# Cross attention layers of a decoder: scores for the row maxima of two heads per step, each head in its own half of the stack's rows; maxima moved in two transfers instead of three

## The reference

```
q = LN(x) @ Wq.T + bq ; k = ctx @ Wk.T + bk ; v = ctx @ Wv.T + bv      (no biases in L0)
scores = einsum('bhqd,bhkd->bhqk', q, k) / sqrt(8)      (L3: masked by a table)
out = softmax(scores) @ v ;  x = x + out @ Wo.T + bo
```

## Time and profile before

| | us |
|---|---|
| runs | 2594.87, 2597.32, 2603.39 |
| median of 3 runs | 2597.32 |
| profiled execution, own time | 2597.72 |
| its span | 2595.9 |
| PE busy | 2275.9 (88%) |
| DVE busy | 1563.2 (60%) |
| ACT busy | 1306.7 (50%) |
| mean granted TensorE clock | 0.933 of full |

### The profile page before, as it was taken

How to read it: one execution, slowest core, us unless ns; L and a number is a source line. 1 busy time by engine, 2 the same in 40 slices (tenths; PEclk the granted TensorE clock), 3 DMA queues, 4 the chain that set the end, 5 groups by cost and what they waited for, 6 DMA issues and landing times. The chain is left out here.

```text
span 2595.9 us, 48375 instructions
## 1 busy us (share of the span) xinstructions
PE 2275.9 (88%) x16585; PEld 1478.1 (57%) x16585; DVE 1563.2 (60%) x4614; ACT 1306.7 (50%) x3591; POOL 722.2 (28%) x996
## 2 busy tenths in 40 slices
PE   8879997789898599976889998887779999899989
PEld 5635544755555245543756766566747776466643
DVE  5667762246666778745366664553366775877730
ACT  5646661235556166652356676422235565466632
POOL 2232202444432522200633231234421121322100
PEclk8989998879999699997989999988989999899999
DMA  2123316220000133220600000265410001232100
GB/s 80 31 71 102 97 41 199 46 65 34 18 34 17 50 100 105 83 84 29 157 3 2 1 1 15 84 137 147 135 37 2 10 2 40 84 86 80 52 19 17
DMA packets 127203, 155.40 MB, mean 60 GB/s; under 512 B 22496, under 2 KB 90345, under 8 KB 125810
## 3 DMA queue, kind: packets, MB, share of 16 engines
q1 hardware_dynamic: 116850, 143.20, 19.3%
q0 software_dynamic: 7488, 7.78, 1.4%
q10 hardware_dynamic: 2624, 1.32, 0.3%
HBM read 117.96 MB, written 34.99 MB: 59 GB/s over the span
## 5 line engine op out<-in xcount | busy, mean ns | idle before, releaser
L540 ACT ACTIVATE L3x_p_ring<-L3x_ps_t 128x512 f32<-128x512 f32 x256 | 141.7, 599 | 101.2 <-PE L3x_ps_t L615 100.1
L442 DVE CUSTOM_DVE_ANT_0 L3x_ps_s<-L3x_ps_s,L3x_mask_q 128x512 f32<-128x512 f32 x256 | 170.1, 718 | 27.6 <-PE L3x_ps_s L596 26.3
L540 ACT ACTIVATE L1x_p_ring<-L1x_ps_t 128x512 f32<-128x512 f32 x256 | 138.0, 623 | 76.9 <-PE L1x_ps_t L613 76.8
L540 ACT ACTIVATE L0x_p_ring<-L0x_ps_t 128x512 f32<-128x512 f32 x256 | 138.0, 626 | 72.7 <-PE L0x_ps_t L613 72.6
L445 DVE TENSOR_REDUCE L0x_mx<-L0x_ps_s 128x2 f32<-128x1024 f32 x128 | 151.9, 1221 | 29.4 <-PE L0x_ps_s L596 29.0
L445 DVE TENSOR_REDUCE L1x_mx<-L1x_ps_s 128x2 f32<-128x1024 f32 x128 | 152.1, 1221 | 21.6 <-PE L1x_ps_s L596 20.4
L1087 ACT ACTIVATE L2a_probs<-L2a_ps_s,L2a_top 128x256 f32<-128x256 f32 x256 | 117.8, 472 | 78.6 <-DVE L2a_top L1022 78.5
L1087 ACT ACTIVATE L3a_probs<-L3a_ps_s,L3a_top 128x128 f32<-128x128 f32 (+1 forms) x256 | 104.0, 422 | 40.1 <-DVE L3a_top L1018 37.9
L613 PE MATMUL L3x_ps_t<-L3x_q_stack,L3x_k_stack 128*128 128x256 bf16 x512 | 120.3, 274 | 1.7 <-DMA L3x_q_stack<-L3x_m_rows 1.4
L615 PE MATMUL L3x_ps_t<-L3x_mask_k,const_ident_bf 128*128 128x256 bf16 x512 | 119.9, 274 | 0.0
L596 PE MATMUL L1x_ps_s<-L1x_k_stack,L1x_q_stack 125*128 125x512 bf16 x256 | 80.6, 397 | 16.3 <-PEq L98 11.8
(11 more groups left out here) (769 smaller groups left out, 6056.0 us busy)
## 6 DMA issues: line engine op xcount, KB each, us to landing
L2f_w_e<-L2f_in_w_e SPq DMA_DIRECT2D x23, 544.0 KB, 3.7
L0f_w<-L0f_in_w SPq DMA_DIRECT2D x32, 256.0 KB, 6.9
L1a_rk_wide<-L1a_rk_dram SPq DMA_DIRECT2D x8, 1024.0 KB
L1f_w<-L1f_in_w SPq DMA_DIRECT2D x32, 256.0 KB, 3.4
L0x_k_stack<-L0x_k_dram SPq DMA_DIRECT2D x84, 96.0 KB
L1x_k_stack<-L1x_k_dram SPq DMA_DIRECT2D x84, 96.0 KB
L3x_k_stack<-L3x_k_dram SPq DMA_DIRECT2D x84, 96.0 KB
kept_x<-ctxT SPq DMA_DIRECT2D x24, 256.0 KB, 3.2
```

Of the source, the lines that this page charges most:

```text
L442: last = dve.tensor_tensor_reduce(span, span, mask_q[:, t, :], 1.0, 2 * MASKED, ALU.add, ALU.max, accum_out=mx[:, t, k:k + 1])
L540: act.activation(p_ring[:, u % RING, j * BANK:(j + 1) * BANK], t_bank(o), ACT.Exp, scale=scale).then_inc(out["t"].sem, 1)
```

## The change

Heads are taken in pairs (h, h+4), one of an even quarter and one of an odd quarter. An even quarter's nine pairs of parts stay in rows 0 to 71, in another order, so that rows 0 to 63 hold all but the product of the two small parts. An odd quarter's stand in rows 56 to 127, so that rows 64 to 127 hold all but that product. Step `s` is now one t of two heads: a matmul over rows 0 to 63 and one over rows 64 to 127, both 128 by 512. There are as many of them. The maxima of an odd quarter's heads go into rows 0 to 2. `t` is as before.

```diff
+Q_SLOTS = (0, 1, 2, 0, 1)
+K_SLOTS = (2, 0, 1, 2)
+STACK_ROWS = (((0, 1, 1), (24, 2, 1), (48, 0, 1)), ((56, 2, 0), (80, 0, 0), (104, 1, 0)))
+MAX_ROWS = (P - 3, 0)
+
+def store_parts(eng, name, dram, parts, stored):
+    if name == "q":
+        eng.dma_start(dram[0:3].rearrange("i p k -> p i k"), parts[:]).then_inc(stored, 16)
+        eng.dma_start(dram[3:5].rearrange("i p k -> p i k"), parts[:, 0:2, :]).then_inc(stored, 16)
+    else:
+        eng.dma_start(dram[1:4].rearrange("i p k -> p i k"), parts[:]).then_inc(stored, 16)
+        eng.dma_start(dram[0:1].rearrange("i p k -> p i k"), parts[:, 2:3, :]).then_inc(stored, 16)
+
+def load_quarter(eng, name, stack, dram, par, quarter, stacked):
+    heads = slice(QUARTER * quarter, QUARTER * (quarter + 1))
+    for row, q_slot, k_slot in STACK_ROWS[quarter % 2]:
+        slot = q_slot if name == "q" else k_slot
+        eng.dma_start(stack[row:row + 24, par, heads], dram[slot:slot + 3].rearrange("i (d h) k -> (i d) h k", h=16)[:, heads]
+                      ).then_inc(stacked, 16)
...
-        m_stacked = [tally(f"m_stacked_{j}_", 3 * 16) for j in range(2)]
+        m_stacked = [tally(f"m_stacked_{j}_", 2 * 16) for j in range(2)]
...
-                        for i in range(3):
-                            sp.dma_start(q_stack[MAX_ROW + i:MAX_ROW + i + 1, par, heads],
-                                         m_rows[H * i + HALF * k:H * i + HALF * (k + 1), k]).then_inc(m_stacked[k].sem, 16)
+                        for odd in range(2):
+                            first = HALF * k + QUARTER * odd
+                            sp.dma_start(q_stack[MAX_ROWS[odd]:MAX_ROWS[odd] + 3, par, first:first + QUARTER],
+                                         m_rows[3 * QUARTER * odd:3 * QUARTER * (odd + 1), k]).then_inc(m_stacked[k].sem, 16)
...
-                        if k % QUARTER == 0 and b == 0:
-                            pe.wait_ge(prologue.stacked[k // QUARTER], 6 * 16)
-                        elif k % QUARTER == 0:
-                            wait_tally(pe, stacked[k // QUARTER], b, 6 * 16)
-                        for t in range(QT):
-                            last = pe.matmul(s_bank(o)[:, t, :], q_stack[0:MAX_ROW, par, k, t * P:(t + 1) * P], k_stack[0:MAX_ROW, par, k, :],
+                        for quarter in (k // QUARTER, k // QUARTER + 1):
+                            if k % HALF == 0 and b == 0:
+                                pe.wait_ge(prologue.stacked[quarter], 6 * 16)
+                            elif k % HALF == 0:
+                                wait_tally(pe, stacked[quarter], b, 6 * 16)
+                        first, t = first_of_pair(k), k % 2
+                        for j in range(2):
+                            rows, h = slice(j * P // 2, (j + 1) * P // 2), first + QUARTER * j
+                            last = pe.matmul(s_bank(o)[:, j, :], q_stack[rows, par, h, t * P:(t + 1) * P], k_stack[rows, par, h, :],
                                              start=True, stop=True)
...
-                            last = pe.transpose(t_bank(o).bitcast(BF16)[:, t * P:(t + 1) * P],
-                                                mparts[:, t, :, :].rearrange("p a h -> p (a h)"), const["ident_bf"][:])
+                            last = pe.transpose(t_bank(o).bitcast(BF16)[0:3 * HALF, t * P:(t + 1) * P],
+                                                mparts[:, k].rearrange("p c i h t -> p (c i h) t")[:, :, t], const["ident_bf"][:])
```

More of the change, by code:

```diff
@@ L268, in attention_cross @@
         v = sb("v", [P, 2, KT, H, 32])
[L269 to L272, removed]
+        mx = sb("mx", [P, 2, 2, QUARTER, QT])
+        mrest = sb("mrest", [P, 2, 2, QUARTER, QT])
+        mparts = sb("mparts", [P, 2, 2, 3, QUARTER, QT], BF16)
+        m_rows = sb("m_rows", [3 * HALF, 2, S], BF16)
         p_ring = sb("p_ring", [P, RING, 2 * BANK])
@@ L329, in load_stack @@
         def load_stack(eng, name, quarter, b):
[L331 to L337, removed]
+            stack, dram, stored = (q_stack, q_dram, q_stored) if name == "q" else (k_stack, k_dram, k_stored)
+            wait_tally(eng, stored, b, 32)
+            load_quarter(eng, name, stack, dram, b % 2, quarter, stacked[quarter].sem)
         with nc.Block() as block:
@@ L452, in _ @@
                             wait_tally(dve, full["m"], b, 0)
[L453 to L454 removed]
                         else:
                             wait_tally(dve, full["m"], b, 1)
[L457 removed]
+                        part = [mparts[:, k, :, i] for i in range(3)]
+                        dve.tensor_scalar(part[0], mx[:, k], -1.0, None, ALU.mult).then_inc(m_steps.sem, 1)
                         wait_tally(dve, m_steps, b, 4 * k + 1)
[L459 to L462 removed]
+                        dve.scalar_tensor_tensor(part[1], mx[:, k], -1.0, part[0], ALU.mult, ALU.subtract).then_inc(m_steps.sem, 1)
+                        dve.scalar_tensor_tensor(mrest[:, k], mx[:, k], -1.0, part[0], ALU.mult, ALU.subtract).then_inc(m_steps.sem, 1)
                         wait_tally(dve, m_steps, b, 4 * k + 3)
[L464 removed]
+                        dve.tensor_tensor(part[2], mrest[:, k], part[1], ALU.subtract).then_inc(m_steps.sem, 1)
                     if kind == "v" and qk_bias:
@@ L544, in _ @@
                         wait_tally(act, m_stacked[k], b, 0)
-                        act.activation(m_rows[:, k], t_bank(o).bitcast(BF16)[:, 0:S], ACT.Copy).then_inc(out["m"].sem, 1)
+                        act.activation(m_rows[:, k], t_bank(o).bitcast(BF16)[0:3 * HALF, 0:S], ACT.Copy).then_inc(out["m"].sem, 1)
                     if kind == "outputs":
@@ L657, in __init__ @@
         self.q_dram = nc.dram_tensor(name + "first_q_dram", [5, P, S], BF16)
-        self.k_dram = nc.dram_tensor(name + "first_k_dram", [3, P, KX], BF16)
+        self.k_dram = nc.dram_tensor(name + "first_k_dram", [4, P, KX], BF16)
         self.masks = masks
     def load_stack(self, eng, name, quarter):
-        heads = slice(QUARTER * quarter, QUARTER * (quarter + 1))
-        dram = self.q_dram if name == "q" else self.k_dram
-        for a in range(3):
-            rows = dram[a:a + 3] if name == "q" else dram[:]
-            eng.dma_start(self.stacks[name][24 * a:24 * a + 24, 0, heads], rows.rearrange("i (d h) k -> (i d) h k", h=16)[:, heads]
-                          ).then_inc(self.stacked[quarter], 16)
+        load_quarter(eng, name, self.stacks[name], self.q_dram if name == "q" else self.k_dram, 0, quarter, self.stacked[quarter])
 def attention_rows(nc, x_sb, const, w, cfg, ahead, follow, stacks, opening, prologue):
@@ L3614, in fill @@
                 def fill(name, par):
-                    rows = prologue.stacks[name][P // 2:P, par].rearrange("p h k -> p (h k)").bitcast(F32)
+                    rows = prologue.stacks[name][:, par].rearrange("p h k -> p (h k)").bitcast(F32)
                     words = two_ones if name == "k" else const["zero"]
-                    act.activation(rows, words[P // 2:P, 0:1].broadcast_to(list(rows.shape)), ACT.Copy).then_inc(filled, 1)
+                    act.activation(rows, words[:, 0:1].broadcast_to(list(rows.shape)), ACT.Copy).then_inc(filled, 1)
                 act.wait_ge(two_made, 1)
```

45 lines of the change are left out of this document (18 added, 27 removed).

## The result

The changed kernel took 2590.94 us (median of 11 runs, 2588.54 to 2593.77), the kernel before beside it 2597.19 (11 runs, 2593.71 to 2603.39). The ratio is 0.9981, 95% interval 0.9972 to 0.9989: 5 to 6 us less (4.9 by the ratio, 6.3 by the medians). The interval tells this from no change, though it is under the 0.3% that the prediction took as its bound. The profiled execution took 2589.7, its span is 2587.8 and its mean clock 0.936. The prediction had said 2590.0.

What follows compares the result with a forecast made beforehand. TensorE was taken to bound L3x throughout, TensorE and VectorE by turns L0x and L1x, with starts at reduced clock. Savings 2.2 + 2.7 + 2.7 = 7.6 us from 2597.7 gave 2590.1, stated as 2590.0; range 2586 to 2594.

Steps and rivals of the forecast that it cites:

- L0x and L1x: Steady batches of these layers: gain counts only where VectorE waits for TensorE; 0.17 us a batch, 2.7 us for 16.
- the starts: Layer starts at half clock: 1.35 us saved up to the first t, 1.3 behind it; together 2.7, bounds 0 and 5.
- L3x's gain: Steady batches of L3x, all TensorE: 0.27 us a batch saved, times 8 is 2.2 us; bounds 1.4 and 3.0.
- Step s: Between full-shape blocks, shape changes included: 0.42 us against 0.435, about 0.01 saved; right behind values 0.115 saved.
- free leaving: Rival: leaving the small shape costs nothing, each s saves 0.09 more; 21 us more, 2569 or part of it; chance 0.20.
- the full 2x: Rival: no change of shape costs; L3x saves 27 us, the others 21; some 2549; chance 0.05.
- the pair's weights: Rival: weights of the pair in s aren't hidden, 0.10 us more each; slower, 2616 to 2628; chance 0.09.
- m's way out: From m's 24-row transposes into t: 0.10 us or nothing; half taken, 0.05 each, two a batch.
- The clock: Layers' starts: a differing clock would prove the forecast wrong; rival that it rises later, 2597 to 2612, chance 0.08.
- The stack's quarters: First s of a half waits for two quarters' loads, expected free; the forecast is wrong if TensorE waits for one.
- Nothing comes through: Rival: in L0x and L1x the gain becomes longer waits for mparts and ScalarE; 2594 to 2600; chance 0.18.

Runs made afterwards that it cites:

- m_full: Changed kernel with m's transposes 128 columns wide again (24 of maxima, the rest zeros): 2589.01 us, ratio to the kernel before 0.9971.
- late_max: Changed kernel with one maximum a batch, the one waiting for the s right behind values, also waiting for the t that follows: 2593.29 us.
- before_m_first: Kernel before, with only the maxima's transfers issued by SP ahead of the six loads of a stack's quarter: 2594.46 us.
- after: The changed kernel in its first profile, no further edit: the profiled execution took 2589.7 us.
- after_again: The changed kernel profiled once more, no edit: 2594.84 us.

## Why the prediction was right, and where it wasn't

The time was right to a microsecond (2590.0 for 2590.94), the saving less so (7.6 for 5 to 6; the base was 0.5 above the later median), and the sum behind it least. Predicted were 2.2 for L3x, 2.7 for L0x and L1x, 2.7 for the starts. The traces give 0.2 for L3x behind its first `y`, 4.8 for L0x and L1x behind theirs, and 1.2 for the three starts up to it, which hold one and a half batches. L3x's gain did not come, L0x's and L1x's was nearly twice as large, and the starts' was half. That these errors of both signs nearly cancelled is luck.

- **Step s, right.** Predicted were 0.42 against 0.435, measured 0.426 against 0.435, and behind `values` 0.115 less predicted, 0.113 measured. The changes of shape eat the gain: free leaving (each step 0.09 cheaper) and the full 2x are out by L3x, whose period didn't fall, and the pair's weights are hidden for a bf16 follower (the next `t` comes 0.32 behind the pair and not 0.42).
- **m's way out, the term that was mis-sized.** Between 0.10 and nothing the prediction took half; it is 0.096, in full, as m_full shows. The price of nothing came from the earlier trace rows, from a group of fp32 transposes, which did not hold for these bf16 ones. The lower bound, 1.4 for L3x, was still too high, because of the next point.
- **x and v behind the pair, not in the sum.** The prediction priced what follows `s` by the `t` that follows; twice a batch it is a fp32 matmul. That a first fp32 matmul behind a change of shape can be 0.10 dearer stood in the earlier trace rows, and the prediction weighed it as a rival for the bf16 pair alone. With it L3x adds up: `s` 14 x 0.009 + 2 x 0.113 = 0.35 less; `m` twice 0.096 and 0.01 for the `t` behind it, 0.21 more; `x` 0.05 and `v` 0.10 more. Together that is +0.01, against +0.02 measured (33.117 to 33.133).
- **L0x and L1x, right mechanism, too small.** 0.17 a batch predicted, 0.32 and 0.33 measured. The step that failed is that `m` costs 2 x 0.05 there: m_full shows that it costs nothing. Without it the prediction's own terms give 0.27, and 0.05 of the 0.32 stay unexplained. VectorE's start behind the `s` that follows `values` came 0.21 earlier (predicted 0.22), and late_max shows that this start passes into the period. In both profiles of before L1x had one batch of 29.4 too. The changed kernel's have none, but neither has before_m_first, so this needn't be the change's doing; it is 0.4 of the 4.8.
- **The starts, half.** From the first `x` to the first `t` 0.45 less was predicted for each layer. L0x has 0.19, L1x 0.08, L3x 0.93 more. In L0x, by the rows above, k's second store is issued 0.40 behind the first (predicted 0.45), and from the maxima's issue to `t` it is 0.88 less (164.21 to 168.07 in the earlier trace rows, 166.22 to 169.20 now; predicted 0.7). But the `s` in the chain didn't shorten it (k's store stands 10.29 behind `x` in both), and the three loads of q took 1.50 instead of 1.18. In L3x it is the second store, here on SP's timeline:

```profile
2216.25 0.49 SPq L81 DMA_DIRECT2D L3x_k_dram<-L3x_k_parts  x1
2219.84 1.12 SPq L89 DMA_DIRECT2D L3x_k_stack<-L3x_k_dram  x3
```

  It is 3.59 from the store's issue to the first load, against 2.53 in L0x. That differs between executions: in after, after_again, m_full and late_max, whose SP lists are the same there, it is 3.59, 3.39, 2.92 and 2.53, and L3x's start is 19.78, 19.59, 19.16 and 18.74. So the start follows this landing, within 0.03 us; why the landing varies stays open. The wait of the first `t` in L0x was to be under 3.17 and is 3.42; it varies as well (3.63 in after_again, 3.13 in late_max). At half clock a step costs 0.54 from `s` to `t`, against 0.86. The way in comes on top: 169.20 to 170.14 is 0.94, for four `t` that stream 0.86, as the two matmuls of the earlier trace rows do, so 0.08. In all it is 0.62, where 0.63 was predicted:

```profile
170.14 0.61 PE L621 MATMUL L0x_ps_s<-L0x_k_stack,L0x_q_stack 64*128 64x512 bf16 x2
170.68 1.04 PE L638 MATMUL L0x_ps_t<-L0x_q_stack,L0x_k_stack 128*128 128x256 bf16 x4
```

- **The clock, left open.** The prediction said that it is wrong if the layers' clock differs. In L0x's first 30 us it is 0.66, before and after. In the same stretch of L1x (from 6 us ahead of its first `x`) it is 0.64 before and 0.56 after:

```profile
890.00:920.00 30.00, 18.77 (x63) 7.44 (x64) 23.14 (x38) 6.86 (x13) 13.36 (x15) 0.64 0.26 74
```

```profile
884.00:914.00 30.00, 17.29 (x61) 6.25 (x62) 22.92 (x38) 6.46 (x11) 13.10 (x14) 0.56 0.28 79
```

  In L3x it is 0.72 and 0.66. The second profiles say the same, 0.61 and 0.56 in L1x, 0.72 and 0.68 in L3x, but late_max, whose starts are the changed kernel's, has 0.63 and 0.72. L1x's first `t` comes 18.5 behind `x` at 0.56 and at 0.63 alike, so no time is seen to hang on it up to there. That the change lowers this clock is neither shown nor excluded.
- **The stack's quarters, right.** In the changed kernel's profile TensorE has no wait for a load of a stack's quarter.
- **Nothing comes through** is out too: `m` does wait longer (0.29 for 0.20), but the gain came through in L0x and L1x, and it was L3x, the layer bound by TensorE, that got nothing.

## What to carry to other kernels

A small shape between large ones is priced by its neighbours: two changes of shape cost here nearly what two concurrent matmuls of 512 columns save (0.20 for 0.22), and a fp32 neighbour behind costs more. Look for an order in which steps of one shape stand side by side (behind `values`, where the way in was paid anyway, `s` saved 0.11), or leave a tiny step in the large shape though it writes more rows. Where engines take turns, look for the start that an engine waits for once a batch, and for work that stands in front of a due transfer in the same queue: such places gave 0.22 us a batch in L0x and 1.6 to 2.2 us a layer's start here, while the halved streaming gave nothing in L3x, where TensorE is busy throughout. And where untouched parts vary by microseconds, compare periods of steady batches, not spans.

## What the runs showed of the hardware

- A change of TensorE's shape costs 0.096 us at full clock each way (109 to 205 ns and 55 to 151 ns between starts), with the first bf16 matmul behind it 0.01 longer; a transpose writing 24 rows is such a change, and costs 0.096 on leaving.
- Behind a bf16 pair of 64 rows the first fp32 matmul takes 0.05 (a transpose of 128 columns, 165 for 113 ns) or 0.10 (the first of `v`, 213 for 111 ns) longer, on top.
- The two matmuls of a pair start 3 ns apart.
- The same kernel's attention part L1a took 364.6 and 369.9 us in two executions, while the periods of other parts repeat to 0.01, but for a batch now and then (one of four in L1x, 29.4 for 29.0).
- A small store's landing can differ between executions: from the issue of k's second store to the first load of L3x it was 2.53 to 3.59 us in four executions of the same list of transfers.
